# A graph network with a routed expert layer on one core: nine output slots in place of three for the experts' rows, and no unread product in each expert segment

## What is computed

```python
    def _L0_ffn_ref(x, router_w, router_b, W1, b1, W2, b2):
        B, K, D = (512, 16, 256)
        E = 32
        H = int(D * 0.25)
        xf = x.reshape(-1, D)
        logits = xf @ router_w.T + router_b
        idx = jnp.argmax(logits, axis=-1)
        w1t = jnp.take(W1, idx, axis=0)
        h = jnp.einsum('nd,ndh->nh', xf, w1t) + jnp.take(b1, idx, axis=0)
        h = jax.nn.relu(h)
        w2t = jnp.take(W2, idx, axis=0)
        out = jnp.einsum('nh,nhd->nd', h, w2t) + jnp.take(b2, idx, axis=0)
        out = jax.nn.relu(out)
        return out.reshape(x.shape)
...
    x = x + _L0_ffn_ref(_layernorm(x, axis=-1)[None], L0_ffn_router_w, ...)[0]
```

## Time and profile before

| what | value |
|---|---|
| runs | 3072.39, 3080.54, 3084.48 us; median 3080.54 |
| profiled execution | 3077.36 us |
| its span, first to last instruction | 3075.2 us |
| mean granted TensorE clock over the span | 0.938 |
| busy over the span | PE 2715.3, DVE 2125.2, POOL 1723.8, ACT 1528.0 us |
| transfers over the span | 207.87 MB, mean 68 GB/s |

### The profile page before, as it was taken

One profiled execution on the slowest core, in us unless ns is written; L12 is line 12 of the kernel. 1 busy time (PEld: TensorE's weight loads), 2 busy tenths in 40 slices (PEclk: granted clock), 3 DMA queues, 4 the chain that ended last, 5 costly groups with the idle time before them and its releaser, 6 DMA issues.

```text
span 3075.2 us, 56118 instructions
## 1 busy us (share of the span) xinstructions
PE 2715.3 (88%) x18842; PEld 2482.9 (81%) x18842; DVE 2125.2 (69%) x4836; ACT 1528.0 (50%) x2947; POOL 1723.8 (56%) x1611
## 2 busy tenths in 40 slices
PE   4888899999979999997999999788888888992597
PEld 2666799999978999996889999688888888992465
DVE  8887567677756666675567767688888886893144
ACT  0333366666635566662565666344444445771254
POOL 0011178777758888885888885154454553224455
PEclk7898899999989999998999999799999998996688
DMA  3000223323232223223223221233323322201332
GB/s 119 24 27 25 82 50 68 68 61 64 54 93 66 63 68 65 59 62 95 64 59 68 65 64 43 64 108 84 87 81 87 82 81 60 59 25 50 85 100 76
DMA packets 255488, 207.87 MB, mean 68 GB/s; under 512 B 165433, under 2 KB 194314, under 8 KB 255205
## 3 DMA queue, kind: packets, MB, share of 16 engines
q1 hardware_dynamic: 197606, 162.55, 19.7%
q0 software_dynamic: 57600, 41.75, 7.0%
HBM read 136.93 MB, written 70.16 MB: 67 GB/s over the span
## 4 chain that ended last, share of the span: by engine, by line
PE 18%; POOL 13%; issue 8%; DVE 7%; DMA 4%; ACT 2%; DVEq 1%; SPq 0%; POOLq 0%; ACTq 0%
PE bank L375 16%; POOL edges_sorted L725 8%; DMA nodes_out<-orow,oidx 3%; POOL tokens_sorted L790 2%; DVE xh L1266 2%; PE bank L1808 1%; DVE hidh_lo L1302 1%; DMA staging<-in_edge_attr 1%; POOL r L703 1%; DVE oh L1494 1%; POOL ehl L742 1%; DVE bn L1257 1%; ACT hidh_hi L837 1%; ACT ehl L913 1%; ACT hid L831 0%
## 5 line engine op out<-in xcount | busy, mean ns | idle before, releaser
L725 POOL DMA_INDIRECT edges_sorted<-staging,pos_i x850 | 1058.2, 1245 | 254.2 <-issue 230.8
L831 ACT ACTIVATE hid<-bank,b1p 128x250 f32<-128x250 f32 x800 | 331.9, 466 | 388.0 <-PE bank L375 385.8
L375 PE MATMUL bank<-h_hi,w_hi 128*128 128x250 f32 x1600 | 482.7, 302 | 19.7 <-DVE h_lo L1286 19.7
L1302 DVE TENSOR_TENSOR hidh_lo<-hid,hidh_hi 128x500 fp32r<-128x500 f32 x400 | 296.9, 742 | 272.6 <-ACT hidh_hi L837 265.1
L375 PE MATMUL bank<-w_hi,hidh_hi 128*125 128x256 f32 x1600 | 468.1, 293 | 0.0
L375 PE MATMUL bank<-h_hi,w_lo 128*128 128x250 f32 x1600 | 451.1, 282 | 0.0
L375 PE MATMUL bank<-w_hi,hidh_lo 128*125 128x256 f32 x1600 | 450.9, 282 | 0.0
L375 PE MATMUL bank<-w_lo,hidh_hi 128*125 128x256 f32 x1600 | 449.8, 281 | 0.0
L375 PE MATMUL bank<-h_lo,w_hi 128*128 128x250 f32 x1600 | 448.0, 280 | 0.0
L375 PE MATMUL bank<-wqk,h 128*125 128x256 f32 x1600 | 380.6, 392 | 0.6 <-ACT mbc L882 0.6
L375 PEld LDWEIGHTS bank<-wqk,h 128*125 128x125 f32 x1600 | 306.3, 195 | 47.4 <-issue 1.2
(11 more groups left out here) (289 smaller groups left out, 5754.5 us busy)
## 6 DMA issues: line engine op xcount, KB each, us to landing
staging<-edges_sorted SPq DMA_DIRECT2D x103, 260.0 KB, 2.7
staging<-in_edge_attr SPq DMA_DIRECT2D x50, 531.2 KB
queries<-qn SPq DMA_DIRECT2D x100, 250.0 KB
qin<-queries SPq DMA_DIRECT2D x100, 250.0 KB
edges_sorted<-staging,pos_i POOLq DMA_INDIRECT x850, 3.7
rows_in<-edges_sorted SPq DMA_DIRECT2D x50, 260.0 KB, 2.7
yin<-tokens_sorted SPq DMA_DIRECT2D x81, 127.0 KB
raw<-in_L_mix_W SPq DMA_DIRECT2D x8, 1024.0 KB, 6.3
```

Source lines behind the costliest of these rows:

```text
L375: return nc.tensor.matmul(o, left, right, start=start, stop=stop, skip_group_check=True)
L725: nc.gpsimd.indirect_dma_start(out=edges_sorted, out_offset=bass.IndirectOffsetOnAxis(ap=pos_i[:, i:i + 1], axis=0), in_=stage[:, slot, j, ...
L831: a = nc.scalar.activation(hid[c % 2][:, j, :], chunks(PH[c % 2])[:, j, :], ACT.Gelu, bias=b1p[:, 2 * c + j:2 * c + j + 1])
L1302: nc.vector.tensor_tensor(hidh[c % 2][1][:, :, :], hid[c % 2][:, :, :], f32(hidh[c % 2][0][:, :, :]), ALU.subtract).then_inc(f_lo, 1)
```

## The change

It does three things.

1. `OUTS` goes from 3 to 9: `orow` and `oidx` have nine buffers each, with nine semaphores. DVE's wait before `oidx` is now for the transfer of segment n - 9. 81 segments are 9 x 9, so the waits at the end on POOL are nine, each for a count of 9.
2. The `idle_product` at the end of each of PE's turns in the segments is gone. The 48 before the segments stay.
3. So that the semaphores suffice, the loads of the experts' rows count on the same 12 semaphores (`ROWS_IN`) as the loads of the edges' rows did before them; the first six have been used by edges, and `tokens_in` adds what those have counted. An unused helper (`segments`) goes.

```diff
-IDLE_SEGMENT = 1
...
-OUTS = 3
+OUTS = 9
...
-        S_IN = [ctx.enter_context(nc.semaphore(f"s_in{i}")) for i in range(RIN)]
+
+        ROWS_IN = [ctx.enter_context(nc.semaphore(f"rows_in{i}")) for i in range(YIN)]
...
-        F_IN = [ctx.enter_context(nc.semaphore(f"f_in{i}")) for i in range(YIN)]
...
-        f_row, f_idx, f_out0, f_out1, f_out2 = sems("f_row f_idx f_out0 f_out1 f_out2")
+        f_row, f_idx = sems("f_row f_idx")
+        F_OUT = [ctx.enter_context(nc.semaphore(f"f_out{i}")) for i in range(OUTS)]
...
+        def edges_in(n):
+
+            return ROWS_IN[n % RIN], 16 * (n // RIN + 1)
+
+        def tokens_in(n):
+
+            slot = n % YIN
+            return ROWS_IN[slot], 16 * (len(range(slot, ESEGS, RIN) if slot < RIN else ()) + n // YIN + 1)
...
-                sp.dma_start(yin[n % YIN][:, :], tokens_sorted[bass.ds(first, P), :]).then_inc(F_IN[n % YIN], 16)
+                sp.dma_start(yin[n % YIN][:, :], tokens_sorted[bass.ds(first, P), :]).then_inc(tokens_in(n)[0], 16)
...
-                    act.wait_ge(F_IN[i % YIN], 16 * (i // YIN + 1))
+                    act.wait_ge(*tokens_in(i))
...
-                    dve.wait_ge(F_IN[n % YIN], 16 * (n // YIN + 1))
+                    dve.wait_ge(*tokens_in(n))
...
-                for _ in range(IDLE_SEGMENT):
-                    idle_product()
```

More of the change, by code:

```diff
@@ L365, in build @@
         n_z, n_zT, n_zTs, n_log, n_top, rw_T, rw_ready = sems("n_z n_zT n_zTs n_log n_top rw_T rw_ready")
-        F_IN = [ctx.enter_context(nc.semaphore(f"f_in{i}")) for i in range(YIN)]
         f_bias, f_ones, f_scat, f_z = sems("f_bias f_ones f_scat f_z")
         f_T, f_zT, f_w1, f_h, f_hTs, f_o = sems("f_T f_zT f_w1 f_h f_hTs f_o")
-        f_row, f_idx, f_out0, f_out1, f_out2 = sems("f_row f_idx f_out0 f_out1 f_out2")
+        f_row, f_idx = sems("f_row f_idx")
+        F_OUT = [ctx.enter_context(nc.semaphore(f"f_out{i}")) for i in range(OUTS)]
         ATTR, SCATTERED = [attr0, attr1], [scattered0, scattered1]
-        N_IN, F_OUT = [n_in0, n_in1], [f_out0, f_out1, f_out2]
+        N_IN = [n_in0, n_in1]
         def mm(o, left, right, start, stop):
@@ L495, in load_segment @@
             eng.dma_start(rows_in[n % RIN][:, :, :],
-                          edges_sorted[bass.ds(first, SEG), :].rearrange("(p r) c -> p r c", r=SEGR)).then_inc(S_IN[n % RIN], 16)
+                          edges_sorted[bass.ds(first, SEG), :].rearrange("(p r) c -> p r c", r=SEGR)).then_inc(edges_in(n)[0], 16)
         block_ = ctx.enter_context(nc.Block())
@@ L733, in seg_low @@
                     nc.gpsimd.memset(agg[:, :, :], 0.0).then_inc(s_ones, 1)
-                pool.wait_ge(S_IN[n % RIN], 16 * (n // RIN) + 16)
+                pool.wait_ge(*edges_in(n))
                 if n >= 4:
@@ L909, in seg_hi @@
                     act.wait_ge(q_out, 16 * ALL)
-                act.wait_ge(S_IN[n % RIN], 16 * (n // RIN) + 16)
+                act.wait_ge(*edges_in(n))
                 if n >= 4:
```

## The result

The change made the kernel slower: 3096.62 us (3092.47 to 3099.83, median of seven runs) against 3081.6 us (3072.39 to 3084.48) for the kernel before in the same measurement, a ratio of 1.0054 [1.0042 to 1.0067]. That is only 0.5%, but clear of its interval. The forecast was 3027 us, faster than before, with a range of 3015 to 3072, so the time lies outside the range, and slower than before instead. The profiled execution took 3099.83 us, the longest of the seven.

The account below looks back on a forecast made before the run. The ring of three output slots was taken to bound at full clock, PE at half. First issue 2893.7 + 120.0 of POOL issues + 3.5 issue waits + 4.9 tail = span 3022.1; with 2.2 and 3.2 added, 3027 us, range 3015 to 3072.

Parts of the forecast that it names:

- the slots: Experts' stage, output buffers: with nine, DVE's 67.4 us of waits for earlier output transfers to land would go.
- (c): Rival for the experts' stage: transfers in flight slow each other or the loads and set the pace; 3051 us, chance 0.07.
- (d): Rival for the experts' stage: the unread product is all, the slots nothing; 2.16 us a segment stays, 3077 us, chance 0.02.
- the paces of PE and the first issue: Experts' stage: PE's turn without the product 1.37 us at full clock, 2.49 at half; first output issued at 2893.7.
- POOL's 1.50 as the pace: Experts' stage at full clock: POOL's output issues, 1.50 us apart, would bound; 80 of them make 120.0 us.
- The 3.5 us for issue waits: Experts' stage: allowance beside POOL's floor, a third of the issue waits of 5.9 us on ACT and 4.8 on PE.
- All but the first are waits for a slot, and those go: PE busy 1.37 of 1.50 has no such stretch: Experts' stage: of the half-busy PE stretches before clock falls, only the one at the stage's start would remain.
- the 0.66 for a full clock throughout: Chance given to the main case: TensorE's clock full through the experts' stage, 3027 us, bounds 3024 to 3035.
- Without it the same mix gives fewer products per us and may not win the clock back at all: Experts' stage at half clock: without the unread product, 0.43 us of each 2.92, full speed may not return.
- rival (a): Half clock from the stage's start to the end: PE bounds at 2.49 us a segment, span 3099, 3105 us, chance 0.14.
- the start's one in four: Start of the experts' stage, where the second load is awaited: clock cut there in one execution in four.
- the ring of three slots: Kernel before, experts' stage: reuse of three output buffers was taken to bound at full clock, 2.16 us a segment.

Follow-up runs that it names:

- e1: The changed kernel with the unread product put back at the end of each turn, nine slots kept: 3029.35 us, ratio 0.9877 to the kernel before.
- g2: Nine slots with the unread product in each turn, run again on another chip: 3033.5 us, ratio 0.9865 to the kernel before.
- g4: The changed kernel with the unread product in every second turn of PE, nine slots: 3034.82 us, ratio 0.9887 to the kernel before.
- e3: The changed kernel without the expert number's register reads on PE and ACT, output not the reference's: median 3064.06 us of ten, ratio 0.9948 from the seven shortest.
- g1: The changed kernel as it stands, run again on another chip: 3096.21 us, ratio 1.0063 to the kernel before.
- f1: The changed kernel with one burst of 16 unread products in PE's turn 40: 3099.61 us, ratio 1.0071 to the kernel before; its profiled execution took 3083.78 us.
- e2: The kernel before without the unread product in the segments, three slots kept: 3088.05 us, ratio 1.0074 to the kernel before.
- f4: The changed kernel with the unread product back in each turn and five slots in place of nine: 3049.1 us, ratio 0.9908 to the kernel before.
- e4: The changed kernel with an unread product of 64 columns each turn: 3028.93 us, ratio 0.9878 to the kernel before, from three executions; the fourth took 3113.34 us.
- f2: The changed kernel with an unread product of 64 x 64, weights of 64 columns too, each turn: 3051.71 us, ratio 0.9926 to the kernel before.
- f3: The changed kernel with two whole unread products at the end of each turn: 3053.26 us, ratio 0.9928 to the kernel before.

## Why the prediction was wrong, step by step

**Right: the slots.** All 67.4 us of waits for a landed transfer are gone, longer landings are hidden, and e1 and g2 are 1.2 and 1.4% below the kernel before. Rivals (c) and (d) did not occur: at a DMA share of 0.45 and 130 GB/s the median landing was 0.4 us longer.

**Right: the paces of PE and the first issue.** 1.37 us a turn at the full clock, 2.49 at half, and 12.7 us from the first load to the first issue are all measured as forecast. The first issue comes as early with the product in the turn (12.5 us in e1), so this gain is the clock's at the start, not the edit's.

**Not reached: POOL's 1.50 as the pace.** The changed kernel ran 7 of 80 segments at the full clock. Where the clock held, with the product, PE set the pace at 1.61, against the 1.59 forecast for that case. In g4 the median came down to 1.50, but the mean only to 1.58. The 3.5 us for issue waits were short: the forecast took 0.8 us as the longest, from the rows of PE and ACT. The same list (the kernel before, from 2884 on) has a row for PE's weight loads, the first of which stand directly behind the read of the number:

```profile
PEld bank L375 <- issue: 38.7, 74, 1.9
```

The forecast left it out, and did not open the durations of the reads, whose tail of 1.4 us is in the kernel before.

**The step that failed: "All but the first are waits for a slot, and those go: PE busy 1.37 of 1.50 has no such stretch".** From this came the 0.66 for a full clock throughout. The stretches before were slot waits with others mixed in. Before the fall near 2920, PE waited first for a read of the number (of 1.37 us, at 2913.5) and then for the slot, as its timeline in the kernel before shows:

```profile
2915.30 0.61 PE L375 MATMUL bank<-zsT,w1s 128*64 128x125 f32 x4 [0.53 <-issue]
...
2917.98 0.69 PE L375 MATMUL bank<-fw,hsT 65*125 x2 [1.48 <-DVE orow L1800]
```

The others stay: in the changed kernel a stretch with PE busy 4.30 of 7.00 us came from two long reads and a late ACT; in e3 it came from a late load; in g1 from the start. A mean of 1.37 of 1.50 us is no guard against single stalls. The prediction looked at how the average turn would be filled, where one gap in 81 turns is enough if nothing brings the clock back.

**Right, and given too little: "Without it the same mix gives fewer products per us and may not win the clock back at all".** That sentence states what happened. It was priced correctly in rival (a), 3099 us of span and slower by 0.8%, and given 0.14 because the chance of a fall was thought to be the start's one in four alone. In three profiled executions of the changed kernel or of it with the burst (the first, f1, g1), and in e2's, the clock fell before 2911 and did not come back by the segments' own work. The executions without a profile agree: the 13 of the changed kernel have mean clocks of 0.916 to 0.928, where the kernel before has 0.938 to 0.948. The edit did two things, which the forecast weighed for a fall at the start only. It removed what brings the clock back: before, and in f4, each fall healed, and in the five profiles without the product (the first, g1, f1, e2, e3) none did without the burst. And it made a fall more likely: with nine slots and an unread product in the turn the clock did not fall in any of six profiles (e1, g2, e4, f2, f3, g4), with six to twelve long reads each, and in those five it always fell. A smaller or rarer product is less sure: of the executions without a profile, one of e4 and one of g4 lost the clock by their means. The first is shown by e2 and f1; for the second the runs show the count, and that the stretches with a stall are fuller with the product (e1), but not what exactly decides a fall.

**The size.** The first profile has 7 segments at 1.37 and 73 at 2.49 in place of 80 at 1.50: 191.3 - 120.0 = 71.3 us more, of which the forecast had 3.5 as issue waits, so 67.8. With the stage's start 7.3 us later and the tail 0.9 longer (5.8 us from 3092.3 to the end, forecast 4.9) that makes 76.0 us, by which the span passed the forecast (3098.1 against 3022.1).

**The sign of the whole.** On one chip the slots alone give 1.2% less and the product's removal alone 0.7% more; both together give 0.5 to 0.6% more (on two other chips). The effects don't add to −0.5%, since at half clock PE's 2.49 us a turn is slower than the ring of three slots was, and the slots' gain has nothing left to act on.

## What to carry to other kernels

Work that nothing reads may be what keeps or returns TensorE's clock: before it is taken out, ask what would bring the clock back after the next stall, and find each stall by the longest of its kind, not by the mean. Read the mean granted clock of every execution too: here it settles what became of those that had no profile. When two edits stand in one change, price each with the other absent and present: the slots are worth 1.2 to 1.4% with the product and nothing that shows without it. A stage in which PE is busy 100% at PEclk 0.50 is a sign to try unread products, here one in every turn at 0.22 us each.

## What was not expected of the hardware

- A PE that the profile shows busy for 179.40 of 179.40 us stayed at half clock (1.2 GHz), while 16 products of 128x128 behind 65 us of half clock brought 2.4 GHz within 3.2 us (f1, its profiled execution).
- The register read of one number takes 0.30 us in the median and now and then 0.9 to 2.1 us, on PE as on ACT (1.2 us there in the changed kernel). Which reads are long differs by execution. In the profiles with half clock nearly throughout (the changed kernel, g1, e2) two of PE's 81 are over 0.9 us, in those at the full clock (e1, g2, g3, e4, f2, f3, g4) six to fourteen. The cause was not sought and stays open, as does ACT's late start of hsT.
- The cost of an unread product does not follow its size: 0.22 us with 128 columns, 0.23 with 64 (weights of 128 columns both), and 0.45 with weights of 64 columns (f2).
